# Layer 1's rotated queries and keys from regrouped weights, in one stage with the expert tiles; the values' products in the route stage

## What is computed

```
xn = layernorm(x)
q, k, v = (xn @ qkv_w.T) split in 3 x 16 heads x 64
q, k: halves t1, t2 (32 wide) of each head -> [t1*c - t2*s, t1*s + t2*c]     # c, s: cos and sin by position
attn = softmax(q k^T / 8 - p * log1p(a * |i - j|)); s = (attn v) @ out_w.T
router: probs = softmax(xn @ Wr + br); expert = argmax; gate = max
y = relu(xe @ W1[expert] + b1[expert]) @ W2[expert] + b2[expert]           # xe = affine layernorm(xn)
x = x + s * silu(y * gate)
```

## Time and profile before

| | us |
|---|---|
| median of 3 runs (range) | 3077.13 (3074.41 to 3077.42) |
| the profiled execution's own time | 3079.59 |
| its span in the trace | 3077.9 |

### The profile page before, as it was taken

How to read it: one execution, slowest core, us unless ns; L and a number is a source line. 1 busy time by engine, 2 the same in 40 slices (tenths; PEclk the granted TensorE clock), 3 DMA queues, 4 the chain that set the end, 5 groups by cost and what they waited for, 6 DMA issues and landing times. The chain is left out here.

```text
span 3077.9 us, 46733 instructions
## 1 busy us (share of the span) xinstructions
PE 2807.8 (91%) x17656; PEld 1147.6 (37%) x17656; DVE 2504.0 (81%) x3379; ACT 1557.4 (51%) x1889; POOL 2502.6 (81%) x1205
## 2 busy tenths in 40 slices
PE   5959999999999999996499599999999999999997
PEld 3413333333333333333354133333333333333332
DVE  6568888888888888874339699999999999999995
ACT  4325555555555555552122255555555555555554
POOL 0009999999999999994339389999999999999997
PEclk9979999999999999997699699999999999999998
DMA  4250111111111111101203501111111111111100
GB/s 109 86 191 22 35 29 28 28 28 28 28 28 28 28 29 28 28 1 38 60 27 137 190 4 52 55 55 55 55 55 55 55 55 55 55 55 55 55 1 14
DMA packets 63825, 155.28 MB, mean 50 GB/s; under 512 B 18017, under 2 KB 33770, under 8 KB 61426
## 3 DMA queue, kind: packets, MB, share of 16 engines
q1 hardware_dynamic: 62578, 150.20, 17.4%
q0 software_dynamic: 1024, 2.10, 0.2%
HBM read 113.34 MB, written 38.93 MB: 49 GB/s over the span
## 5 line engine op out<-in xcount | busy, mean ns | idle before, releaser
L943 POOL TENSOR_TENSOR a_sums<-a_sums,room 128x1024 f32<-128x1024 f32 x512 | 1195.4, 2364 | 83.1 <-ACT room L795 42.5
L699 PE MATMUL a_ov<-room,va 128*64 128x512 f32 x4096 | 994.0, 606 | 0.0
L784 ACT ACTIVATE room<-room,sscale 128x1024 f32<-128x1024 f32 x512 | 588.3, 1149 | 539.3 <-DVE room L878 539.2
L845 DVE TENSOR_REDUCE a_mx<-a_jb 128x1 f32<-128x1024 f32 x501 | 611.9, 1221 | 129.6 <-PE a_jb L653 123.4
L943 POOL TENSOR_TENSOR a_sums<-room 128x1024 f32<-128x1024 f32 x256 | 604.3, 2361 | 116.6 <-ACT room L784 66.8
L840 DVE CUSTOM_DVE_ANT_0 a_junk<-a_jb,a_tab 128x1024 bf16<-128x1024 f32 x501 | 610.5, 1219 | 83.2 <-PE a_jb L653 74.8
L878 DVE TENSOR_TENSOR room<-a_st,a_tab 128x1024 f32<-128x1024 f32 x512 | 622.9, 1217 | 12.4 <-PE a_st L688 10.2
L795 ACT ACTIVATE room<-a_st,sscale 128x1024 f32<-128x1024 f32 x256 | 285.3, 1114 | 360.1 <-PE a_st L688 360.1
L652 PE MATMUL a_jb<-a_kh,a_qh 64*128 64x512 f16 x1002 | 384.9, 384 | 66.1 <-DVE a_mx L840 32.1
L699 PEld LDWEIGHTS a_ov<-room,va 128*64 128x64 f32 x4096 | 248.7, 136 | 409.3 <-issue 372.7
L688 PE MATMUL a_st<-a_qh,a_kh 64*128 64x512 f16 x2048 | 395.6, 383 | 3.0 <-DVE a_mx L840 2.9
(11 more groups left out here) (219 smaller groups left out, 2642.6 us busy)
## 6 DMA issues: line engine op xcount, KB each, us to landing
a_tab<-bias_line SPq DMA_DIRECT2D x16, 1984.0 KB, 11.0
qk_high<-q_oh SPq DMA_DIRECT2D x32, 512.0 KB, 2.6
qk_low<-q_ol SPq DMA_DIRECT2D x32, 512.0 KB, 3.6
a_qh<-qk_high SPq DMA_DIRECT2D x64, 256.0 KB, 4.5
a_kh<-qk_high SPq DMA_DIRECT2D x64, 256.0 KB, 5.1
a_ql<-qk_low SPq DMA_DIRECT2D x64, 256.0 KB, 7.5
a_kl<-qk_low SPq DMA_DIRECT2D x64, 256.0 KB, 7.8
ex_w<-in_L_ffn_W SPq DMA_DIRECT2D x1, 2048.0 KB, 10.5
```

The source lines that it names most:

```text
L699: last = nc.tensor.matmul(ov[t * DH:(t + 1) * DH, :], k.va[:, 2 * s + t, h * DH:(h + 1) * DH], prob[:, step % RING, t * QC:(t + 1) * QC], ...
L784: nc.scalar.activation(prob[:, r, :], prob[:, r, :], ACT.Exp, scale=k.sscale[:, layer:layer + 1])\
L845: nc.vector.reduce_max(mx[:, j // 2, j % 2:j % 2 + 1], scratch(n, j), AX.X).then_inc(max_done, 1)
L943: nc.gpsimd.tensor_tensor(a, first, prob[:, step % RING, :], ALU.add).then_inc(summed, 1)
```

## The change

The expert stage and the query and key part of the qkv stage become one stage, `experts_and_rotation_stage`; the values move into the route stage; the gathers and Silu move to the beginning of the attention stage.

- Weights of queries and keys are regrouped (by POOL, in the route stage) so that 128 columns hold one 32-wide half of four heads. One product gives the first halves of four heads, a second one the other halves, and `wsw` and its products are gone: 16 jobs of 4 matmul calls in place of 32 jobs of 4. A job's four rotated products are four DVE multiplications, two POOL instructions, two roundings on ACT and two subtractions on DVE.
- A job writes 32-row pieces of four heads, so the stores to `qk_high` and `qk_low` are four for each job, with a destination of 4 pieces of 32 rows of 1024 numbers.
- The eight experts' weights are no longer all loaded. SP reads each tile's expert number and fetches that expert's W1 and W2 (256 KB each) to one of three places.
- ReLU with bias and the copy of results are ACT's alone.
- `work[j]` gives the expert tiles that stand behind job j in the lists of PE, ACT and SP: jobs 1 to 14 have 2, 2, 1, 2, 2, 1, 2, 2, 1, 2, 2, 1, 2, 1 tiles, jobs 0 and 15 none. The two PSUM parts of a job are single: PE may not write one before DVE has read it for the job before.

```diff
@@ attention_stage, ACT, before the first exponent
+                act.wait_ge(gathered, 16 * NT)
+                for q in range(NT):
+                    nc.scalar.activation(k.gate[:, q, :], k.gate[:, q, :], ACT.Silu, scale=k.prob[:, q:q + 1])
@@ attention_stage, POOL, after the memsets
+                for q in range(NT):
+                    nc.gpsimd.indirect_dma_start(k.gate[:, q, :], None, k.sorted_out[:, :],
+                                                 bass.IndirectOffsetOnAxis(ap=k.spot[:, q:q + 1], axis=0))\
+                      .then_inc(gathered, 16)
@@ route_stage
-            sp.dma_start(w1[:, :, :], t["L1_ffn_W1"].rearrange("e m f -> m e f")).then_inc(weights_loaded, 16)
+            for i in range(2):
+                for r in range(2):
+                    nc.gpsimd.tensor_copy(grouped[:, i, r, :, :], halves[:, i, :, r, :])
...
+            def values_of(q):
+                if q >= 2:
+                    pe.wait_ge(val_copied, q - 1)
+                for c in range(2):
+                    last = nc.tensor.matmul(val[:, q % 2, c * QC:(c + 1) * QC], k.xnT[:, q * P:(q + 1) * P],
+                                            k.w1[:, 2, c * QC:(c + 1) * QC], start=True, stop=True)
+                last.then_inc(valued, 1)
...
+            for q in range(NT):
+                act.wait_ge(valued, q + 1)
+                nc.scalar.activation(k.va[:, q, :], val[:, q % 2, :], ACT.Copy).then_inc(val_copied, 1)
@@ experts_and_rotation_stage, SP
+            def pick(i):
+                owner = sp.value_load(tiles[0:1, i:i + 1], min_val=0, max_val=NE - 1)
+                if i >= 3:
+                    sp.wait_ge(dn_done, i - 2)
+                sp.dma_start(wts[:, i % 3, 0, :], t["L1_ffn_W1"][bass.ds(owner, 1)].rearrange("a m f -> (a m) f"))\
+                  .then_inc(picked[i % 3], 16)
...
+            def store_qk(j):
+                g, i, half = jobs[j]
+                sp.wait_ge(low, 2 * j + 2)
+                for n, store in enumerate((k.qk_high, k.qk_low)):
+                    rows = store[i].rearrange("a p s -> (a p) s").rearrange("(g h r d) s -> g r h d s", g=4, h=4, r=2)
+                    for r in range(2):
+                        sp.dma_start(rows[g, r, :, :, half * 1024:(half + 1) * 1024], split[:, j % 2, n, r, :])\
+                          .then_inc(stored[j % 2], 16)
...
+            for j in range(NJOB + 2):
+                if j >= 2:
+                    store_qk(j - 2)
+                for i in work[j - 1] if 1 <= j <= NJOB else ():
+                    if i + 3 < TL:
+                        pick(i + 3)
@@ the same, PE
+            def project(j):
+                g, i, half = jobs[j]
+                for r, (part, ready) in enumerate(((low_part, a_ready), (high_part, b_ready))):
+                    if j >= 1:
+                        pe.wait_ge(prod, 4 * (j - 1) + 2 * r + 2)
+                    for c in range(2):
+                        q0 = half * 1024 + c * 512
+                        last = nc.tensor.matmul(part[:, c * 512:(c + 1) * 512], wqk[:, i, r, g * P:(g + 1) * P],
+                                                k.xnT[:, q0:q0 + 512], start=True, stop=True)
+                    last.then_inc(ready, 1)
@@ the same, ACT
+            def high_halves(j):
+                if j >= 2:
+                    act.wait_ge(stored[j % 2], 64 * (j // 2))
+                for r, rotated in enumerate((first, second)):
+                    act.wait_ge(rot, 2 * j + r + 1)
+                    nc.scalar.activation(split[:, j % 2, 0, r, :], rotated[:, j % 2, :], ACT.Copy).then_inc(high, 1)
@@ the same, POOL
+                pool.wait_ge(prod, 4 * j + 3)
+                nc.gpsimd.tensor_tensor(first[:, b, :], first[:, b, :], product[:, 0, :], ALU.subtract).then_inc(rot, 1)
+                pool.wait_ge(prod, 4 * j + 4)
+                nc.gpsimd.tensor_tensor(second[:, b, :], second[:, b, :], product[:, 1, :], ALU.add).then_inc(rot, 1)
```

More of the change, by code:

```diff
@@ new lines, in experts_and_rotation_stage @@
+        high, low, stored = m.sem("er_high"), m.sem("er_low"), [m.sem("er_stored0"), m.sem("er_stored1")]
+        xs_loaded, turned, xs_copied = m.sem("er_xs_loaded"), m.sem("er_turned"), m.sem("er_xs_copied")
+        spread, b1_copied, picked = m.sem("er_spread"), m.sem("er_b1_copied"), [m.sem(f"er_picked{b}") for b in range(3)]
+        up_done, relu_done, dn_done, y_copied, y_stored = (m.sem("er_up_done"), m.sem("er_relu_done"), m.sem("er_dn_done"),
+                                                           m.sem("er_y_copied"), m.sem("er_y_stored"))
@@ L1173, in expert_tiles_stage, with xs, xsT @@
         block = ctx.enter_context(nc.Block())
         NG = (TL + 3) // 4
+        jobs = [(g, i, half) for g in range(4) for i in range(2) for half in range(2)]
+        NJOB = len(jobs)
+        work = [[i for i in range(TL) if 1 + i * (NJOB - 2) // TL == j] for j in range(NJOB)]
         def members(g):
             return range(4 * g, min(4 * g + 4, TL))
+        def xs(a, b):
+            return k.acc[:, a:b, :] if b <= NT else xs_more[:, a - NT:b - NT, :]
+        def xsT(a, b):
+            return xsT_first[:, a:b, :] if b <= NT else xsT_more[:, a - NT:b - NT, :]
@@ new lines, in downward @@
+            def downward(i):
+                o = dn[:, i % 4, :]
+                if i % 4 == 0 and i >= 4:
+                    pe.wait_ge(y_copied, i // 4)
+                nc.tensor.matmul(o, hot[:, i:i + 1].broadcast_to([NE, P]), b2[:, :], start=True, stop=False)
+                pe.wait_ge(relu_done, i + 1)
+                for j in range(FT):
+                    last = nc.tensor.matmul(o, hT[:, i % 2, j, :], wts[:, i % 3, 1, j * P:(j + 1) * P],
+                                            start=False, stop=(j == FT - 1))
+                last.then_inc(dn_done, 1)
@@ new lines, in _ @@
+            for j in range(NJOB):
+                if j >= 1:
+                    high_halves(j - 1)
+                for i in work[j]:
+                    if i == 0:
+                        copy_x(0)
+                    if i % 4 == 0 and i // 4 + 1 < NG:
+                        copy_x(i // 4 + 1)
+                    act.wait_ge(up_done, i + 1)
+                    if i >= 2:
+                        act.wait_ge(dn_done, i - 1)
+                    for f in range(FT):
+                        last = nc.scalar.activation(hT[:, i % 2, f, :], up[:, i % 2, f, :], ACT.Relu,
+                                                    bias=b1t[:, f, i:i + 1])
+                    last.then_inc(relu_done, 1)
+                    if i % 4 == 0 and i >= 4:
+                        copy_y(i // 4 - 1)
```

254 lines of the change are left out of this document (129 added, 125 removed).

## The result

The changed kernel takes 3097.0 us (median of 4 runs, 3094.5 to 3099.4) against 3075.8 for the kernel before (median of 4, 3074.4 to 3077.4): a ratio of 1.0069, interval [1.0051, 1.0086], 21 us slower. The forecast was 3068, about 8 us faster. The profiled execution has a span of 3092.7 us and a time of 3094.5, 2.5 under the median of its kernel, where that of before was 3.8 over its own: so the spans differ by 14.8 us only.

The account below looks back on a forecast made before the run. Stores on four DMA engines were to set the merged stage's pace: -239.1 + 227 + 2.0 + 1.4 = -8.7 us from a profiled 3079.6 gives 3070.9, so a median of 3068. The range was 2980 to 3096.

Parts of the forecast that it names:

- Four engines for a store: Merged stage: a store with outermost count 4 gets four DMA engines, always the same, 10.6 us a job.
- The bound of the four engines, 223.8 us: Merged stage: head, 16 jobs at 10.6 us, 20 fetches, five result stores and 1.0 us at the end, 223.8 us.
- For gaps on the four engines that follow from it I add 3: Merged stage: low clock at first and expert tiles waiting for fetches behind stores cost 3 us, making 227.
- so in between the engines don't run dry: Merged stage: two output places let DVE and POOL finish a job during the previous job's store; no size given.
- DVE 7.2 us and POOL 6.5 us a job: Merged stage: DVE's six instructions take 7.2 us a job, POOL's two at 3.27 take 6.5 us.
- First rival: Merged stage: stores spread over all engines, PE and DVE set the pace, stage 143 us, median 2984; chance 0.22.
- Slower rival, PE loses its clock: Merged stage: PE works in bursts at the low clock, stage 252 us, total 3093; chance 0.12.
- 2 KB rows dearer: Merged stage: stores of 2 KB rows cost more, 14.1 us a job, stage 283, total 3124; chance 0.08.
- Route stage +2.0: Route stage: products of three value tiles ahead of the ranking cost 2.0 us, bounds 0 and +6.
- Attention +1.4: Attention's start: gathers running beside the loads PE waits for cost 1.4 us; Silu and table load stay hidden.
- What would show it: Signs, mainly in the merged stage: late stores, DMA share 0.3 to 0.4, ACT waiting for stored buffers, PE for fetches.
- about 40 us for three jobs and five tiles: Merged stage: expected sign, a period of about 40 us for three jobs and five tiles.

Follow-up runs that it names:

- e10: Changed kernel with a fourth place for an expert's weights, so that a fetch is issued one tile earlier: 3066.1 us, ratio 0.9969.
- the short addition: Changed kernel with POOL's addition and subtraction on 64 of 1024 columns, so work is left out: 3078.7 us, ratio 1.0011.
- the stores by head with both other edits: Changed kernel with one head's rows per store, a fourth place for weights, and an order keeping POOL away from DVE's subtraction: 2986.7 us.
- e9: Fastest version (stores by head, fourth weights place, POOL kept from DVE's subtraction) with the ranking's products ahead of all values' products: 2994.4 us.

## Why the prediction was wrong, point by point

- *Four engines for a store*: right, shown in both directions (shares 0.96, 0.26 and 0.13 for counts of 32, 4 and 2). 10.5 us a job measured, 10.6 forecast. What carried over is the rate of one moving engine, 25 GB/s in the kernel before (262 over 0.66 x 16) and with four; with all engines at once it is 16, so that the 2.64 us from which the 10.6 was made is itself wrong (4.1). The page "DMA: Bandwidth & Descriptors" of the Trainium skill, section "Why a DMA increments its semaphore by 16 and not by 1", has this rule, and says that such a queue takes the lowest-numbered engines. The trace agrees with the rule; of the second it shows only that queued stores don't spread to further engines (two busy with eight stores queued), not which engines they are.
- *The bound of the four engines, 223.8 us*: right, its last 2 us by luck. With the fetch a tile earlier the stage takes 224.0; but there the first store is issued 20.4 us after the stage's start (1491.99 to 1512.34) and not 17.1, and 19 fetches follow it instead of 20. With these two the same sum gives 225.5.
- *"For gaps on the four engines that follow from it I add 3"*, and "so in between the engines don't run dry": **the step that failed.** The four engines stood still for 19 us, and the stage without such holes is 29 us shorter, 224.0 for 253.1. Of the 29, 17 are the holes; in the other 12 the engines are recorded as moving, one fetch (1.55 us by the sum's own term) has gone ahead of the first store, and the rest was not resolved. I had counted what a fetch takes from the engines and not what it costs to stand behind the stores. SP issues it late as well, because a place must be free. PE, which works in order, waits 67 us for eight fetches; behind it stand the next job's products, behind these DVE and POOL, and behind these the stores. The loop closes on the engines that were said to be the bound. The sign of the forecast hung on this: with the holes at about 2 us (e10) the time is 3066.1, a ratio of 0.9969 to before, beside my 3068.
- *DVE 7.2 us and POOL 6.5 us a job*: wrong, 10.4 together. I read from the earlier trace rows that POOL slows from 2.35 to 3.27 us beside a subtraction, and left DVE at 1.22. In the changed kernel the two don't slow each other a little, they take turns: POOL runs 1585.31 to 1587.66, DVE's subtraction started at 1586.27 ends at 1588.73, 1.07 after it; POOL's second, started at 1587.61, ends at 1590.94, 2.21 after that; DVE's second ends at 1592.03, 1.09 after that. With all engines it cost 26 to 35 us; on four engines with the fourth place nothing (3066.1 against 3067.0). What it cost in the changed kernel itself is not shown: the short addition's 16 us hold a shorter POOL as well, and POOL's order with three places was not run. The page "SBUF — State Buffer" of the Trainium skill, section "SBUF: two separate sides", says that DVE with two SBUF inputs and a GpSimd instruction that reads SBUF take a shared port pair for a whole instruction; the times here agree. By that rule of the page and the rows a job is an estimate of 10.7 us: three products of DVE (3.59), then by turns POOL 2.35, a subtraction 1.20, POOL 2.35, a subtraction 1.20. The rows of the kernel before fit it too: there the subtraction starts first, POOL's instruction of 1636.88 ends 2.22 us after it, and only POOL seems slow:

```profile
1636.72 1.22 DVE L455 TENSOR_TENSOR q_ol<-q_t,q_oh 128x1024 f16<-128x1024 f32 x1
```

- *First rival* (all engines, stage 143, 2984): not what the change does, but it is what the stores by head with both other edits do: stage 143.9, 2986.7. The number holds only with the collision and the late fetches mended; the stores alone give 3042. It is met in part by luck: a job's stores take 4.1 us and not 2.64, and the DMA share in the middle is 0.83, where the rival has the queue half empty.
- *Slower rival, PE loses its clock* (stage 252, 3093): its number is nearly the measured one, its mechanism is not. The clock is 0.72 and PE busy 148 us; but e10 with a clock of 0.76 and PE busy 147 us needs 224.0. The low clock lengthens each hole a little (8 instructions of a tile in 2.08 us after a wait, 1.06 otherwise); how much of the 29 us that is was not separated.
- *2 KB rows dearer*: no; 10.5 us a job, where this rival has 14.1.
- *Route stage +2.0*: +4.7, inside its bounds of 0 to +6. Ranking came 3.9 us later, not 2.7, as the 12 products took 8.39 us and not 6.9, more of them at the low clock:

```profile
1452.71 8.39 PE L1077 MATMUL rt_val<-w,room 128*128 128x512 f32 x12
1460.94 0.28 PE L1085 MATMUL rt_tot<-rt_before,ones 128*128 128x8 f32 x2
```

  But what ends the stage is the values' last copy, which I had under the scatters. The copies end at 1489.7, the last scatter is issued by 1486.3. Most of them start 1.72 us apart; before the 14th, 15th and 16th ACT stood 1.8, 3.9 and 0.4 us, pauses that the forecast did not have (see the end).
- *Attention +1.4*: +0.6. Silu and the table load end at 1777.6, 2.9 us before the first exponent, as forecast.
- *What would show it*: DMA at 0.39 and PE waiting for fetches, ACT for stores (64.5 us): seen. Not seen: "about 40 us for three jobs and five tiles", which took 46 (138.6 for nine jobs) and without the holes 38.5; and the values under the scatters. I named PE's waits for fetches as a sign of the forecast; they were its refutation, and I had not asked who stands behind PE.

## What to carry to other kernels

When stages that need different engines are laid over each other, sum not only each engine's work but walk once around the loop of waits: load, in-order engine, what is queued behind it, store, and back to the load's place in the queue. A resource that is busy 92% of the time can still be held back by such a loop; the test is to move the waiting transfer a step earlier, not only to make it smaller. And look at the outermost count of a store's access pattern: with 32, 4 and 2 the same bytes took 4.1, 10.5 and 21 us a job.

## What the runs showed of the hardware that I had not expected

- DVE's f32 subtraction from two SBUF tiles and POOL's f32 addition exclude each other: 1.22 and 2.35 us alone, 3.37 and 3.33 when each starts under the other, and back at 1.35 and 2.36 when the waits keep them apart. DVE's products from PSUM beside POOL stay at 1.22. The one that started first takes its usual time, and the other ends its own time after that.
- Near the end of the values' products PE and ACT pause in every one of these kernels. In the kernel with the ranking first no copy starts between 1477.2 and 1482.2, while the scatters go on. The view gives "remote" as what ended ACT's wait, and no instruction. The cause was not tested.
- In e9, after PE had stood for 3 us up to 1487.7, the granted clock was at the lower level, 0.50, from 1490 to 1492 while the last values were made, which lengthens its route stage further; a window of it:

```profile
1490.00:1494.00 4.00, 4.00 (x8) 1.74 (x7) 0.00 (x0) 1.86 (x2) 0.00 (x0) 0.68 0.00 0
```
